# Layer-norm statistics, normalised rows and weight-row products computed inside the message join of a two-layer graph network

## What is computed

```python
xn = _layernorm(x)
x = x + _L1_gnn_ref(xn, W1, W2, b, src, dst) + _L1_mix_ref(xn[None], ...)[0]
x = x + _L1_ffn_ref(_layernorm(x)[None], ..., wr, br, w1, b1, w2, b2)[0]

def _L1_ffn_ref(x, ...):            # one row block of 3125 rows here
    weights = (x @ wr + br)[..., 0]  # one number for each row
    k = 3125 // 2
    idx = top_k(weights, k)[:k - 1]  # 1561 rows are chosen
    y = gelu(x[idx] @ w1 + b1) @ w2 + b2
    return x with y * weights[idx] placed on the chosen rows, + x
```

## Time and profile before

| | us |
|---|---|
| median of 3 runs | 3233.11 |
| the execution that was profiled | 3240.4 |
| its span, first to last instruction | 3238.6 |
| TensorE matmul busy in the span | 2536.1 (78%) |
| VectorE busy | 2338.4 (72%) |
| GpSimd busy | 1404.5 (43%) |
| ScalarE busy | 1277.3 (39%) |
| tile loop of the message join, first operand to last residual | 2881.4 to 2947.3 |
| opening of the row choice up to its first key instruction | 2948.2 to 2993.8 |
| rest of the row choice on VectorE | 2993.8 to 3019.1 |

### The profile page before, as it was taken

One profiled execution on the slowest core, in us unless ns is written; L12 is line 12 of the kernel. 1 busy time (PEld: TensorE's weight loads), 2 busy tenths in 40 slices (PEclk: granted clock), 3 DMA queues, 4 the chain that ended last, 5 costly groups with the idle time before them and its releaser, 6 DMA issues. The chain is left out here.

```text
span 3238.6 us, 61561 instructions
## 1 busy us (share of the span) xinstructions
PE 2536.1 (78%) x18415; PEld 1850.8 (57%) x18415; DVE 2338.4 (72%) x4046; ACT 1277.3 (39%) x2919; POOL 1404.5 (43%) x1347
## 2 busy tenths in 40 slices
PE   0496999999999999998363999579999999763192
PEld 0253556655655565555252556469998999752061
DVE  6553888888888888887463876679998989749212
ACT  0142555555555555555021111364454444521020
POOL 1587776667767676673423260440000000152304
PEclk9997999999999999999675999799999999976596
DMA  4225999999999999995224232100000000120202
GB/s 138 53 82 150 274 274 271 266 268 272 264 271 273 268 265 268 268 267 152 50 82 125 92 99 74 50 22 9 11 9 12 11 9 11 29 56 30 62 21 65
DMA packets 251542, 426.95 MB, mean 132 GB/s; under 512 B 58552, under 2 KB 162330, under 8 KB 251263
## 3 DMA queue, kind: packets, MB, share of 16 engines
q0 software_dynamic: 91152, 234.00, 26.2%
q1 hardware_dynamic: 156892, 185.84, 19.9%
q10 hardware_dynamic: 3344, 5.11, 0.4%
HBM read 509.62 MB, written 152.30 MB: 204 GB/s over the span
## 5 line engine op out<-in xcount | busy, mean ns | idle before, releaser
L1105 POOL DMA_INDIRECT edge_kv<-scratch_kv,edge_idx x784 | 832.5, 1062 | 346.2 <-issue 212.7
L1449 PE MATMUL edge_ps_o<-edge_vals,edge_onehot 128*128 128x264 f32 x1568 | 439.8, 403 | 29.3 <-ACT edge_rows L1314 19.9
L2827 PE MATMUL msg_ps_o<-all_fp,msg_at 125*123 125x256 bf16 x3375 | 437.2, 278 | 20.3 <-ACT msg_at L2880 16.8
L1314 ACT ACTIVATE edge_rows<-edge_ps_o 128x264 f32<-128x264 f32 x784 | 292.2, 392 | 292.6 <-PE edge_ps_o L1449 279.9
L1130 DVE TENSOR_TENSOR edge_prod<-edge_ps_q,edge_kv 128x512 f32<-128x512 f32 x392 | 257.5, 687 | 182.5 <-PE edge_ps_q L1364 167.2
L2827 PEld LDWEIGHTS msg_ps_o<-all_fp,msg_at 125*123 125x123 bf16 x3375 | 373.2, 138 | 26.6 <-ACT msg_at L2880 19.8
L1449 PEld LDWEIGHTS edge_ps_o<-edge_vals,edge_onehot 128*128 128x128 f32 x1568 | 259.5, 190 | 192.9 <-ACT edge_rows L1314 139.9
L1239 ACT ACTIVATE edge_hid<-edge_ps_h,edge_b 128x512 f32<-128x512 f32 x392 | 247.9, 684 | 178.9 <-PE edge_ps_h L1333 178.9
L1364 PE MATMUL edge_ps_q<-edge_qw,edge_slots 128*128 128x256 bf16 x2352 | 296.2, 277 | 12.6 <-DMA edge_qw<-scratch_qc 11.6
L2852 POOL TENSOR_TENSOR msg_x<-msg_x,msg_b 125x256 f32<-125x256 f32 x25 | 29.3, 1172 | 616.0 <-PE msg_ps_n L2803 616.0
L2939 DVE TENSOR_TENSOR msg_lom<-all_colb,msg_lo_t 128x1500 bf16<-128x1500 bf16 (+1 forms) x180 | 273.0, 1516 | 22.6 <-PE msg_ps_a L2779 5.1
(11 more groups left out here) (520 smaller groups left out, 4292.6 us busy)
## 6 DMA issues: line engine op xcount, KB each, us to landing
edge_qw<-scratch_qc SPq DMA_DIRECT2D x980, 192.0 KB
scratch_part<-edge_rows SPq DMA_DIRECT2D x196, 396.0 KB
scratch_part<-edge_rows SPq DMA_DIRECT2D x196, 132.0 KB
edge_ef<-in_edge_t_dram SPq DMA_DIRECT2D x98, 256.0 KB, 4.1
edge_sgb<-scratch_seg SPq DMA_DIRECT2D x98, 256.0 KB, 5.9
ffn_w<-in_L_ffn_w_dram SPq DMA_DIRECT2D x18, 1024.0 KB, 9.1
edge_kv<-scratch_kv,edge_idx POOLq DMA_INDIRECT x784
scratch_kv<-tab_kvrow SPq DMA_DIRECT2D x25, 250.0 KB
```

Of the source, the lines that this page charges most:

```text
L1105: pool.indirect_dma_start(kv[p][:, t, :], None, K.kv_d, bass.IndirectOffsetOnAxis(ap=idx[p][:, t:t + 1], axis=0)).then_inc(rows_in[p][q], 16)
L1314: act.activation(rows[q % 2][:, t, :], ps_o[t % 2][:, 0:RW], ACT.Copy).then_inc(row_ready, 1)
L1449: pe.matmul(ps_o[t % 2][:, 0:RW], onehot[q % 2][:, t, :], vals[q % 2][:, t, :], start=True, stop=True).then_inc(out_done, 1)
L2827: m = pe.matmul(ps_o[gl % 3][0:GR, 0:D], at[gl % 3][:, h, :], K.fp[:, h, k, :], start=h == 0 and k == 0, stop=h == NT - 1 and k == 2)
```

## The change

Statistics, normalisation and products with wr leave the opening of `route_topk` and go into the tile loop of `join_messages`. `measure` and `spread` follow each residual at once. `normalise` runs six iterations behind the residual and writes over `K.xrow`, which is the own row of the tile and has been used by then (so `xall` is no longer a tile of its own). The multiplication with wr goes to GpSimd, one instruction for each tile in place of one for each group; its outputs lie in the tiles that the first part of the join has done with. The sum stays on VectorE, per group. ScalarE takes the root per group. GpSimd multiplies the first group ahead of the row gathers of the last group, and the other four groups behind them. In `route_topk` GpSimd adds the normalised rows to `K.x` as soon as its constants are set, and VectorE begins with the keys.

```diff
-        edge0 = sb("edge0", [EP, EK, D])
+        edge_space = sb("edge_space", [P, EK, D])
+        edge0 = edge_space[0:EP]
...
-        base = sb("base", [EP, EK, D])
+        base_space = sb("base_space", [P, EK, D])
+        base = base_space[0:EP]
+        prod = [x[0:RT, 0:UN, :] for x in (edge_space, base_space)]
+        wr = sb("wr", [RT, D])
...
         @block.sync
...
+            sp.dma_start(wr[:], bcast_row(I["L1_ffn_wr"].rearrange("n o -> (n o)"), RT)).then_inc(w_in, 16)
         @block.gpsimd
         def _(pool):
...
-            pool.memset(base[:], 0.0).then_inc(cleared, 1)
+            pool.memset(base, 0.0).then_inc(cleared, 1)
...
+            def weigh(g):
+                for i in range(g * UN, (g + 1) * UN):
+                    pool.wait_ge(xn_ready, i + 1)
+                    if g >= 2 and i % UN == 0:
+                        pool.wait_ge(dotted, g - 1)
+                    pool.tensor_tensor(prod[g % 2][:, i % UN, :], K.xrow[:, i, :], wr[:], ALU.mult).then_inc(weighed, 1)
             for i in range(NT):
+                if i == NT - UN:
+                    pool.wait_ge(w_in, 64)
+                    weigh(0)
...
                     pool.wait_ge(ab_ready, 2 * (i - UN))
...
                 pool.indirect_dma_start(row[:, i % (2 * UN), :].bitcast(I32), None, K.part1_d,
                                         bass.IndirectOffsetOnAxis(ap=K.startp[:, i, 1:2], axis=0)).then_inc(row_in[i // UN], 16)
+            for g in range(1, NG):
+                weigh(g)
         @block.vector
         def _(dve):
+            dve.memset(eps[:], EPS).then_inc(measured, 1)
...
-            dve.wait_ge(w_in, 48)
+            dve.wait_ge(w_in, 64)
             def operands(i):
...
-            for i in range(NT + 2 + UN + 1):
+            def measure(i):
+                dve.wait_ge(x_ready, i + 1)
+                dve.bn_stats(stats[:, i, :], K.x[:, i, :]).then_inc(measured, 1)
+            def spread(i):
+                dve.wait_ge(measured, 2 * i + 2)
+                dve.bn_aggr(mv[:, i, :], stats[:, i, :]).then_inc(measured, 1)
+            def normalise(i):
+                g = i // UN
+                if i % UN == 0:
+                    c = slice(i, i + UN)
+                    dve.wait_ge(dev_ready, g + 1)
+                    dve.reciprocal(rdev[:, c], dev[:, c]).then_inc(rdev_ready, 1)
+                    dve.wait_ge(rdev_ready, g + 1)
+                dve.tensor_scalar(K.xrow[:, i, :], K.x[:, i, :], mv[:, i, 0:1], rdev[:, i:i + 1],
+                                  ALU.subtract, ALU.mult).then_inc(xn_ready, 1)
+            def dot(g):
+                dve.wait_ge(weighed, UN * (g + 1))
+                dve.tensor_reduce(K.dots[:, g * UN:(g + 1) * UN], prod[g % 2], AX_X, ALU.add).then_inc(dotted, 1)
+            RES = 2 + UN + 1
+            XN = RES + UN + 1
+            for i in range(NT + XN):
...
                     operands(i)
-                j = i - 2
-                if 0 <= j < NT:
-                    embed(j)
-                r = j - UN - 1
-                if 0 <= r and r % UN == 0:
-                    lengths(r // UN)
+                if 0 <= i - 2 < NT:
+                    embed(i - 2)
+                r = i - RES
...
+                    if r % UN == 0:
+                        lengths(r // UN)
                     residual(r)
+                    measure(r)
+                    spread(r)
+                n = i - XN
+                if n >= 0:
+                    if n % UN == 2 and n > UN:
+                        dot(n // UN - 1)
+                    normalise(n)
+            dot(NG - 1)
         @block.scalar
         def _(act):
...
+            def deviations(g):
+                c = slice(g * UN, (g + 1) * UN)
+                act.wait_ge(measured, 2 * UN * (g + 1) + 1)
+                act.activation(dev[:, c], mv[:, c, 1], ACT.Sqrt, bias=eps[:]).then_inc(dev_ready, 1)
             for i in range(NT):
...
+                g = i // UN - 2
+                if g >= 0 and i % UN == UN - 1:
+                    deviations(g)
...
             square(NT - 1)
+            for g in range(NG - 2, NG):
+                deviations(g)
         @block.tensor
         def _(pe):
...
-            pe.wait_ge(w_in, 48)
+            pe.wait_ge(w_in, 64)
...
-        wr = sb("wr", [RT, D])
...
-        xall = sb("xall", [RT, NT, D])
...
-        prod = [sb(f"prod{b}", [RT, UN, D]) for b in range(2)]
-        dots = sb("dots", [RT, NT])
+        xall = K.xrow
+        dots = K.dots
...
         @block.sync
         def _(sp):
-            sp.dma_start(wr[:], bcast_row(I["L1_ffn_wr"].rearrange("n o -> (n o)"), RT)).then_inc(w_in, 16)
...
-            pool.wait_ge(xn_ready, NT)
             pool.tensor_tensor(K.x[:], K.x[:], xall[:], ALU.add).then_inc(summed, 1)
...
         @block.vector
         def _(dve):
-            dve.memset(eps[:], EPS).then_inc(measured, 1)
-            for i in range(NT):
-                dve.bn_stats(stats[:, i, :], K.x[:, i, :]).then_inc(measured, 1)
-            dve.wait_ge(measured, NT + 1)
-            for i in range(NT):
-                dve.bn_aggr(mv[:, i, :], stats[:, i, :]).then_inc(measured, 1)
-            dve.wait_ge(dev_ready, 1)
-            dve.reciprocal(rdev[:], dev[:]).then_inc(measured, 1)
-            dve.wait_ge(measured, 2 * NT + 2)
-            dve.wait_ge(w_in, 32)
-            def normalise(i):
-                dve.tensor_scalar(xall[:, i, :], K.x[:, i, :], mv[:, i, 0:1], rdev[:, i:i + 1],
-                                  ALU.subtract, ALU.mult).then_inc(xn_ready, 1)
-            def weigh(g):
-                dve.wait_ge(xn_ready, UN * (g + 1))
-                if g >= 2:
-                    dve.wait_ge(dotted, g - 1)
-                dve.tensor_tensor(prod[g % 2][:], xall[:, g * UN:(g + 1) * UN, :], wr[:].unsqueeze(1).to_broadcast([RT, UN, D]),
-                                  ALU.mult).then_inc(weighed, 1)
-            def dot(g):
-                dve.wait_ge(weighed, g + 1)
-                dve.tensor_reduce(dots[:, g * UN:(g + 1) * UN], prod[g % 2][:], AX_X, ALU.add).then_inc(dotted, 1)
-            for g in range(NG):
-                for u in range(UN):
-                    normalise(g * UN + u)
-                if g:
-                    dot(g - 1)
-                weigh(g)
-            dot(NG - 1)
-            dve.wait_ge(dotted, NG)
+            dve.wait_ge(w_in, 16)
...
             def also(ins):
...
-        @block.scalar
-        def _(act):
-            act.wait_ge(measured, 2 * NT + 1)
-            act.activation(dev[:], mv[:, :, 1], ACT.Sqrt, bias=eps[:]).then_inc(dev_ready, 1)
         @block.tensor
         def _(pe):
...
         K.weight = sb("weight", [RT, NT])
+        K.dots = sb("dots", [RT, NT])
...
```

More of the change, by code:

```diff
@@ L3030, in join_messages @@
         mask = space[0:EP, :].rearrange("e (k m c) -> e k m c", k=EK, m=EK)
-        base = sb("base", [EP, EK, D])
+        base_space = sb("base_space", [P, EK, D])
+        base = base_space[0:EP]
+        prod = [x[0:RT, 0:UN, :] for x in (edge_space, base_space)]
+        wr = sb("wr", [RT, D])
+        eps = sb("eps", [RT, 1])
+        stats = sb("stats", [RT, NT, 6])
+        mv = sb("mv", [RT, NT, 2])
+        dev = sb("dev", [RT, NT])
+        rdev = sb("rdev", [RT, NT])
         row = space[0:RT, 0:2 * UN * D].rearrange("p (u d) -> p u d", d=D)
@@ L3066, in join_messages @@
         x_ready = sem("x_ready")
+        measured = sem("measured")
+        dev_ready = sem("dev_ready")
+        rdev_ready = sem("rdev_ready")
+        xn_ready = sem("xn_ready")
+        weighed = sem("weighed")
+        dotted = sem("dotted")
         block = ctx.enter_context(nc.Block())
@@ L3233, in route_topk @@
         LV = 15
-        wr = sb("wr", [RT, D])
         br = sb("br", [RT, 1])
         zero = sb("zero", [TKR, 2 * UT, D])
-        xall = sb("xall", [RT, NT, D])
-        eps = sb("eps", [RT, 1])
-        stats = sb("stats", [RT, NT, 6])
-        mv = sb("mv", [RT, NT, 2])
-        dev = sb("dev", [RT, NT])
-        rdev = sb("rdev", [RT, NT])
-        prod = [sb(f"prod{b}", [RT, UN, D]) for b in range(2)]
-        dots = sb("dots", [RT, NT])
+        xall = K.xrow
+        dots = K.dots
         half = sb("half", [RT, NT, 2])
@@ L3272, in route_topk @@
         consts = sem("consts")
-        measured = sem("measured")
-        dev_ready = sem("dev_ready")
-        xn_ready = sem("xn_ready")
-        weighed = sem("weighed")
-        dotted = sem("dotted")
         summed = sem("summed")
```

## The result

| | before | after |
|---|---|---|
| median, same chip | 3235.77 us (3230.43 to 3237.56, 5 runs) | 3253.49 us (3247.50 to 3254.27, 5 runs) |
| profiled execution | 3240.4 | 3254.27 |
| its span | 3238.6 | 3252.4 |

The account below looks back on a forecast made before the run. VectorE was taken to bound the choice's opening and become the join's bound: 28.8 + 8.9 + 2.0 + 4.6 = 44.3 us more, 30.4 less, so 3233.1 becomes 3247.0 us. Own range 3239 to 3257, overall 3237 to 3259.

Parts of the forecast that it names:

- join, VectorE's own work: Join's loop from iteration 8: VectorE's instructions take 76.1 us where there were 47.26, 28.8 more.
- the stop before tile 20: Join: the last five gathers wait behind GpSimd's multiplications, so VectorE stands 8.9 us before tile 20's operands.
- TensorE's clock: Join, after the stop: TensorE restarts at granted clock 0.5, and VectorE waits 2.0 us for its products.
- holds by GpSimd's multiplications: Join: 17 multiplications each hold VectorE's operands, embed or residual for 0 to 0.55 us; 4.6 us taken.
- choice, from its first instruction to line 3370: Opening of the choice: work leaves, but GpSimd's addition holds the first keys; 30.4 us less.
- end of the join's stage: Close of the join's stage: the prediction gave it no cost, 0 us.
- The rival in which TensorE stays slow: Join: TensorE's clock falls from waiting in every iteration, a tile costs about 4.6 us, 29 more: 3276 us; chance 0.05.
- The rival of nothing held: Keys and join's loop: GpSimd holds no small VectorE instructions, 11.8 us return and 4.6 go: 3230.6 us; chance 0.08.
- the one of hidden work: Join's loop: unseen slack shrinks the 28.8 us by 10 or more, the choice's 30.4 win: 3226 us; chance 0.07.

Follow-up runs that it names:

- kernel 7: Kernel before with GpSimd's 6400-element addition moved to the feed-forward stage and only bn_stats moved into the join, one tile behind its residual: 3225.91 us, ratio 0.9968.
- Kernel 6: Kernel after with all gathers first, GpSimd's addition in the feed-forward stage, and the last group's product by wr made by VectorE: 3231.85 us, one run.
- kernel 2: Kernel after with GpSimd's 6400-element addition moved from the row choice to the start of the feed-forward stage: 3733.17 us on a slower chip, ratio 1.0010.
- kernel 1: Kernel after with all 25 gathers issued ahead of GpSimd's first multiplication: 3246.25 us measured again, ratio to the kernel before 1.0024.
- kernel 4: Kernel after with all gathers first and GpSimd's addition moved to the feed-forward stage: 3230.35 us measured again, ratio to the kernel before 0.9979.

## Why the prediction was right

By the steps of the sum, for the profiled executions:

| term | forecast | measured |
|---|---|---|
| join, VectorE's own work (of 76.1 us) | +28.8 | +28.5 |
| the stop before tile 20 | +8.9 | +7.3 |
| TensorE's clock | +2.0 | +0.8 |
| holds by GpSimd's multiplications | +4.6 | +6.3 |
| choice, from its first instruction to line 3370 | -30.4 | -30.0 |
| end of the join's stage | 0 | +2.4 |

- **VectorE's own work.** 90.2 less the other three terms is 75.8 us, where 76.1 were worked out from single steps. It is a remainder and carries the errors of the three. An iteration is 2.64 (forecast 2.66) and 2.94 (3.00) without its hold. That VectorE's work can't hide in this loop was the decisive step, and kernel 7 shows it: the loop could take 2.9 us.
- **The stop.** From the normalisation of tile 4 to the operands of tile 20 it is 11.65 us (forecast 12.5), since a gather follows a multiplication after 0.18 us, where I had taken 0.9 from a released wait. Holds had also made VectorE itself later: 4.39 instead of 3.6.
- **The clock.** After 8.52 us of waiting the transposes took 1.10 us and the products 2.95. The granted clock was 0.50, the lower of the two levels (1.2 GHz), up to 2949.0 and then rose, and VectorE waited only 0.51 us. The forecast had the products slow from end to end. A second fall, which the forecast did not have, cost 0.26. The rival in which TensorE stays slow did not come: the granted clock was 1.00 up to the stop.
- **The holds.** I took the middle of 0 and 0.55 for 17 multiplications. The trace shows 0.47 to 0.48 on nine pairs (4.2), 0.30, 0.30 and 0.26 on two embeds and a residual (0.9), and 1.2 on normalisations, 0.2 of it beside a gather's issue. Those I had not counted among what can be held. So the step was mis-sized at both of its ends: a multiplication does start in time to hold the pair, nearly always, and normalisations are held as well.
- **The choice.** The addition starts 2.15 us after the stage's first constant and the hold ends with it, as forecast. That the key instruction with one tensor input would be the held one, I had only as an aside.
- **The end of the stage.** The forecast had nothing here. GpSimd's last multiplication ends at 2988.0, its drain at 2991.9, and the first constant of the choice comes 3.30 us after VectorE's last instruction instead of 0.87. Kernel 6 takes 2.3 of it away.

The terms missed by -1.6, -1.2, +1.7, +0.4, +2.4 and -0.3, and -1.6 - 1.2 + 1.7 + 0.4 + 2.4 - 0.3 = +1.4, which the -0.6 ahead of the loop and the -0.9 at the end, not of the change's making, take back. That the sum hit the profiled pair to 0.1 us is luck: its errors cancel, and by the medians it is 3.8 us short. That each term lies within 2.4 us of what was measured is not.

The rival of nothing held is refuted by kernel 2, the one of hidden work by kernel 7: 2.9 us are hidden. Its time of 3226 would have needed 21 us, not the 10 that the prediction gives with it. And the upper end of the forecast's own range adds up to 3256.4, not 3257.

## What to carry to other kernels

Before work is moved from a stage where one engine is alone into a loop that "overlaps", take that engine's share of the loop: at 41 of 47 us busy, each microsecond moved in comes out on the path, less the 3 that are free. The time worth having was not the moved work but the 12 us in one row out of line, and one moved GpSimd instruction brings it (0.9956). And giving work to GpSimd is no relief of VectorE while GpSimd reads and writes SBUF beside VectorE's two-input or scalar instructions: 7.4 us handed over cost VectorE as much again, and 2.2 more at the end of the stage.

## What the runs showed of the hardware

- **Which instructions are held.** Beside a GpSimd addition in SBUF, a VectorE instruction of one tensor input and a scalar, 125x25 in fp32, waits to the addition's end (13.45 us in place of 0.23, and 13.36 for two in place of some 0.4), constant or scalar per row alike; sums over one input run through (0.27 for two). A copy of 8 elements is held as well (6.67 in place of 0.16). The Trainium skill (SBUF — State Buffer, section SBUF: two separate sides) names two SBUF inputs or a two-port mode as what is held, and the Trainium skill (VectorE: DVE Perf Modes, section Mode 2×_2P) counts fp32 scalar instructions to that mode. The traces agree with the hold. By the two sections together line 3365 is held and the gain is the 30.1, beside 30.0 measured; the prediction read the first alone, as if it might pass. The traces don't show the mode's speed: 256 elements still step by 0.30 to 0.34 us, no faster than `bn_stats`.
- **GpSimd's drain.** At the end of a stage it took 5.06 and 5.12 us, and ended 3.8 and 3.9 us after GpSimd's last multiplication. It costs nothing where another engine ends later, and 2.2 us where GpSimd's last work lies just ahead of the stage's end.
- **TensorE's clock after short waits.** In the kernel after, it had 2.84 us without work, and the products behind that took 3.10 us in place of 1.89; the granted clock was 1.00 in the wait and 0.50 from 2957.5 to 2959.5. After 2.49 us in kernel 1, they took 3.21. After the 1.48 us between the tiles before, they took 1.89. The length of one wait does not decide alone: in the second execution of kernel 4 the clock stayed at 1.00 after 2.48 us without work and the products took 1.89, and after 2.45 us later in it they took 2.95.

```profile
2935.51 0.65 PE L3275 MATMUL mjoin_psT<-all_ident,mjoin_ab 125*128 125x125 f32 x4 [1.48 <-DVE mjoin_ab L3153]
2935.99 1.89 PE L3286 MATMUL mjoin_psE<-mjoin_w,mjoin_abt 128*125 128x256 f32 x8
2946.41 1.10 PE L3275 MATMUL mjoin_psT<-all_ident,mjoin_ab 125*128 125x125 f32 x4 [8.52 <-DVE mjoin_ab L3153]
2947.30 2.95 PE L3286 MATMUL mjoin_psE<-mjoin_w,mjoin_abt 128*125 128x256 f32 x8
...
2955.25 0.65 PE L3275 MATMUL mjoin_psT<-all_ident,mjoin_ab 125*128 125x125 f32 x4 [2.84 <-DVE mjoin_ab L3153]
2955.74 3.10 PE L3286 MATMUL mjoin_psE<-mjoin_w,mjoin_abt 128*125 128x256 f32 x8
```

- **Several small multiplications in a row hold as one.** In kernel 1 three multiplications, 2.28 us together, held the pair for 1.7 us: VectorE's second instruction does not get in between them.
